# Graph and expert network: the first tile of layer 2 splits its chunks ahead, and layer 1 clamps the rows

## The reference

```
x = x + gnn(layernorm(x));   x = x + ffn(layernorm(x))

gnn(h):  two layers of
    agg[n] = max over the edges (s -> n) of h[s]       # segment_max, 512 wide
    h      = relu(agg @ W_rel.T + b + h @ W_root.T)

ffn(x):  8 experts; each expert takes the 512 nodes with the largest
    softmax(x @ Wr, axis=0), runs gelu(sel @ W1 + b1) @ W2 + b2 (width 256),
    weights the rows and adds them into the output
```

## Time and profile before

| | |
|---|---|
| runs | 989.93, 992.68, 992.88 us; median 992.68 |
| profiled execution | 991.74 us, span of the engines' work 989.9 us |
| busy share of the span | TensorE 70%, VectorE 68%, GpSimd 57%, ScalarE 26% |
| granted TensorE clock, mean | 0.879 of full speed |
| L846, gathers | 372, 393.9 us busy |
| L1165, the sums | 1165 matmuls, 303.3 us busy |
| L899, L910 | 219.2 and 158.1 us busy |
| layer 1, layer 2 (first to last gather) | about 135 to 403 us, 428 to 753 us |

### The profile page before, as it was taken

One profiled execution on the slowest core, in us unless ns is written; L12 is line 12 of the kernel. 1 busy time (PEld: TensorE's weight loads), 2 busy tenths in 40 slices (PEclk: granted clock), 3 DMA queues, 4 the chain that ended last, 5 costly groups with the idle time before them and its releaser, 6 DMA issues.

```text
span 989.9 us, 9615 instructions
## 1 busy us (share of the span) xinstructions
PE 693.8 (70%) x2488; PEld 313.8 (32%) x2523; DVE 674.0 (68%) x1222; ACT 259.1 (26%) x369; POOL 565.9 (57%) x551
## 2 busy tenths in 40 slices
PE   0319286875887888634588858888886414999997
PEld 0215132332333333211143424334433312444442
DVE  3679947888788878635588878888889695231210
ACT  0265151212222221111243314441332100222222
POOL 5655347777777767543156677567667004456533
PEclk9859687997999999785699979998998755999999
DMA  5716537766777766563257777677666604557646
GB/s 139 229 17 211 161 104 207 216 199 186 213 215 205 216 197 201 183 194 113 69 170 214 223 213 239 195 214 238 197 178 178 225 0 111 101 89 116 137 48 80
DMA packets 65780, 164.33 MB, mean 166 GB/s; under 512 B 16592, under 2 KB 20988, under 8 KB 65719
## 3 DMA queue, kind: packets, MB, share of 16 engines
q0 software_dynamic: 41440, 126.86, 47.5%
q1 hardware_dynamic: 17006, 17.17, 6.2%
q10 hardware_dynamic: 7288, 19.76, 6.0%
HBM read 144.44 MB, written 19.18 MB: 165 GB/s over the span
## 4 chain that ended last, share of the span: by engine, by line
PE 39%; DVE 27%; issue 14%; DMA 10%; POOL 4%; ACT 4%; DVEq 2%; POOLq 0%; ACTq 0%; SPq 0%
PE pp L1165 10%; DMA mem<-tab,ic 7%; DVE acc L899 7%; PE pp L1489 6%; PE pp L1476 6%; PE prow L1136 6%; DVE weights L910 6%; PE prow L1103 3%; POOL mem L846 3%; PE prow L1124 2%; DVE mem L1346 2%; PE pp L1487 1%; POOL mem L379 1%; PE prow L520 1%; DVE mem L445 1%
## 5 line engine op out<-in xcount | busy, mean ns | idle before, releaser
L846 POOL DMA_INDIRECT mem<-tab,ic x372 | 393.9, 1059 | 223.0 <-issue 118.1
L1165 PE MATMUL pp<-weights,slots 128*128 128x512 bf16 x1165 | 303.3, 407 | 124.6 <-DVE acc L899 65.6
L899 DVE TENSOR_TENSOR acc<-acc,pp 128x1024 f32<-128x1024 f32 x180 | 219.2, 1218 | 55.0 <-PE pp L1165 48.9
L1165 PEld LDWEIGHTS pp<-weights,slots 128*128 128x128 bf16 x1200 | 117.7, 103 | 313.7 <-issue 114.2
L910 DVE TENSOR_TENSOR weights<-weights,mem 128x1024 f32<-128x1024 f32 x129 | 158.1, 1226 | 18.8 <-DVE weights L910 11.9
L1136 PE MATMUL prow<-weights,aggT 128*128 128x512 f32 x160 | 81.3, 635 | 13.7 <-ACT aggT L1213 13.7
L1528 POOL DMA_INDIRECT out<-mem,node_of x32 | 50.3, 1572 | 69.4 <-ACT mem L1506 67.0
L1457 DVE COPY weights<-prow 128x512 f32<-128x512 f32 x32 | 20.8, 687 | 100.7 <-PE prow L1103 100.7
L1124 PE MATMUL prow<-weights,rootT 128*128 128x512 f32 x160 | 74.0, 605 | 0.0
L1489 PE MATMUL pp<-weights,mem 128*128 128x512 f32 x128 | 63.5, 618 | 0.0
L1476 PE MATMUL pp<-weights 128*128 128x512 f32 x128 | 58.2, 609 | 0.9 <-DVE weights L1457 0.9
(11 more groups left out here) (348 smaller groups left out, 761.2 us busy)
## 6 DMA issues: line engine op xcount, KB each, us to landing
slots<-ttd ACTq DMA_DIRECT2D x20, 640.0 KB, 6.2
mem<-tab,ic POOLq DMA_INDIRECT x372, 3.7
weights<-in_L_ffn_W SPq DMA_DIRECT2D x9, 512.0 KB, 10.7
weights<-in_L_ffn_W ACTq DMA_DIRECT2D x7, 512.0 KB, 4.1
xnd<-xin ACTq DMA_DIRECT2D x10, 256.0 KB, 3.2
mem<-in_x SPq DMA_DIRECT2D x2, 1120.0 KB
tab<-mem SPq DMA_DIRECT2D x1, 2240.0 KB
weights<-in_L_gnn_W_rel SPq DMA_DIRECT2D x2, 1024.0 KB, 12.1
```

The lines of the kernel that those rows point to most:

```text
L846: g.indirect_dma_start(ring[:, h * PAIR + k, :], None, tables[l], bass.IndirectOffsetOnAxis(ic[:, j * PAIR + k:j * PAIR + k + 1], 0))\
L899: v.tensor_tensor(acc[:, :, :], acc[:, :, :], pp[j % 2][:, :, :], ALU.max).then_inc(S["pa"], 1)
L1165: ins = t.matmul(pp[j % 2][:, i, :], sel[u][:, j * KP + i, :], hot[:, j, w, :], start=w == 0, stop=w == 2)
```

## The change

- In layer 2's first tile the loop takes, in round j, what is left of chunk j+3 (`rest`), the third part of chunk j+2 and the maximum of chunk j. Four chunks are begun ahead of it, three of them to the end. The three last gathered pairs are folded after rounds 6, 7 and 8 (before: ahead of maximum 5, ahead of maximum 8, and behind maximum 9).
- The first part is rounded by ScalarE (`high` in `middles`), two chunks ahead of the middle parts.
- The minimum against the largest finite bfloat16 leaves that tile. In layer 1 VectorE does it on the hidden rows (`clamp`), after maximum 2 of the next tile, and writes the clamped rows into `stage`; the tenth clamp stands behind layer 1's last tile. The scatters read `stage` and wait for the clamp (`hc`).
- SP loads the first two blocks of layer 2's index columns ahead of its wait for the scatters.

```diff
@@ SP, per layer
             if l == 0:
                 s.wait_ge(S["xs"], 16 * NQ)
                 after(s, ct, n_wraw)
             else:
+                for b in range(2):
+                    s.wait_ge(s_ic[0][b], (n_pairs_s // LAP) * 16 + 16)
+                    load_indices(0, b)
                 s.wait_ge(S["sc"], 16 * NQ)
...
-            for b in range(2):
-                after(s, ca, n_idx1s[b])
-                if l:
-                    s.wait_ge(s_ic[0][b], (n_pairs_s // LAP) * 16 + 16)
-                load_indices(0, b)
-            after(s, ca, n_idx1)
+            if l == 0:
+                for b in range(2):
+                    after(s, ca, n_idx1s[b])
+                    load_indices(0, b)
+                after(s, ca, n_idx1)
@@ GpSimd, the scatter
-                    g.wait_ge(S["h"], q + 1)
-                    g.indirect_dma_start(tab2, ..., own_row[q], None)\
+                    g.wait_ge(S["hc"], q + 1)
+                    g.indirect_dma_start(tab2, ..., stage[:, q, :], None)\
                         .then_inc(S["sc"], 16)
@@ VectorE
-            def high(c):
-
-                v.wait_ge(s_hx[HGROUP[c]], 32)
-                v.tensor_scalar(hot[0:CN, c, 0, :], stage[0:CN, c, :], TOP, None, ALU.min).then_inc(S["hh"], 1)
+            def clamp(q):
+
+                v.wait_ge(S["h"], q + 1)
+                v.tensor_scalar(stage[:, q, :], own_row[q], TOP, None, ALU.min).then_inc(S["hc"], 1)
+
+            def rest(c):
+
                 v.wait_ge(S["hh"], c + 1)
-                v.scalar_tensor_tensor(stage[0:CN, c, :], stage[0:CN, c, :], TOP, hot[0:CN, c, 0, :], ALU.min, ALU.subtract)\
-                    .then_inc(S["hr"], 1)
+                v.tensor_tensor(stage[0:CN, c, :], stage[0:CN, c, :], hot[0:CN, c, 0, :], ALU.subtract).then_inc(S["hr"], 1)
@@ vec_tile, k == NQ
-                    high(0)
-                    high(1)
+                    rest(0)
+                    rest(1)
                     lowest(0)
-                    high(2)
+                    rest(2)
                     lowest(1)
+                    rest(3)
+                    lowest(2)
                     first_three(k, lo)
-                    pe_pair(k, 1)
-                    for j in range(2, PAIRS):
-                        if j + 1 < NC:
-                            high(j + 1)
-                        lowest(j)
-                        if j == 5:
+                    for j in range(1, PAIRS):
+                        if j + 3 < NC:
+                            rest(j + 3)
+                        if j + 2 < NC:
+                            lowest(j + 2)
+                        pe_pair(k, j)
+                        if j == 6:
                             with v.Fori(3, m) as i:
                                 pool_pair(lo + i)
+                        if j == 7:
+                            pool_pair(lo + m)
                         if j == 8:
-                            pool_pair(lo + m)
-                        pe_pair(k, j)
-                    pool_pair(lo + m + 1)
+                            pool_pair(lo + m + 1)
@@ vec_tile, layer 1, between maximum 2 and maximum 3
+                        if q:
+                            clamp(q - 1)
                         pe_pair(k, 3)
@@ VectorE, behind layer 1's tiles
+            if l == 0:
+                clamp(NQ - 1)
@@ ScalarE
             def middles():
 
-                for c in range(NC):
+                def high(c):
+                    a.wait_ge(s_hx[HGROUP[c]], 32)
+                    a.activation(hot[0:CN, c, 0, :], stage[0:CN, c, :], ACT.Copy).then_inc(S["hh"], 1)
+
+                def middle_part(c):
                     a.wait_ge(S["hr"], c + 1)
                     a.activation(hot[0:CN, c, 1, :], stage[0:CN, c, :], ACT.Copy).then_inc(S["hm"], 1)
+
+                high(0)
+                high(1)
+                for c in range(NC):
+                    middle_part(c)
+                    if c + 2 < NC:
+                        high(c + 2)
```

More of the change, by code:

```diff
@@ L246, in build @@
         names = """x dst small dnx gt gfree gedge gmax edge general w fw fw2 tab src dstf rec recs xs
-            ready done fin rT rTe aT aTe gn h sc xin x2 xn nT nTe lg lge xns bn rc ra fb2 b2 b2l hh hr hm hl nmx exp
+            ready done fin rT rTe aT aTe gn h sc xin x2 xn nT nTe lg lge xns bn rc ra fb2 b2 b2l hc hh hr hm hl nmx exp
             apart_s warm apart_g apart_v out add neg bits bias pairs pa merge mask
@@ L772, in build, with load_indices @@
             features = tables[l][0:N, :].rearrange("n (p j) -> p n j", p=P)
+            def load_indices(i, b):
+                s.dma_start(ic[:, b * SLOTS:(b + 1) * SLOTS], idx1[:, bass.ds((i * 2 + b) * SLOTS, SLOTS)])\
+                    .then_inc(s_ic[l][b], 16)
             if l == 0:
@@ L792, in build @@
                 n_pairs_s = s.value_load(meta1[0:1, NQ:NQ + 1], min_val=NQ * MINP // 2, max_val=NQ * LCAP // 2)
-            def load_indices(i, b):
-                s.dma_start(ic[:, b * SLOTS:(b + 1) * SLOTS], idx1[:, bass.ds((i * 2 + b) * SLOTS, SLOTS)])\
-                    .then_inc(s_ic[l][b], 16)
-            for b in range(2):
-                after(s, ca, n_idx1s[b])
-                if l:
-                    s.wait_ge(s_ic[0][b], (n_pairs_s // LAP) * 16 + 16)
-                load_indices(0, b)
-            after(s, ca, n_idx1)
+            if l == 0:
[3 more added lines that the diff above has]
+                after(s, ca, n_idx1)
             if l:
@@ L860, in build @@
                 for q in range(NQ):
-                    g.wait_ge(S["h"], q + 1)
-                    g.indirect_dma_start(tab2, bass.IndirectOffsetOnAxis(nodeo[:, q:q + 1], 0), own_row[q], None)\
+                    g.wait_ge(S["hc"], q + 1)
+                    g.indirect_dma_start(tab2, bass.IndirectOffsetOnAxis(nodeo[:, q:q + 1], 0), stage[:, q, :], None)\
                         .then_inc(S["sc"], 16)
@@ L1079, in build @@
                 vec_tile(l * NQ + q)
-            if l:
+            if l == 0:
+                clamp(NQ - 1)
+            else:
                 cv.link(v.tensor_scalar(j15[:, :], jji[:, :], J - 1, None, ALU.bitwise_and))
```

## The result

The changed kernel takes 965.21 us (median of four runs, 964.32 to 965.55) where the kernel before takes 992.54 (four runs); the ratio is 0.9729, 95% interval 0.9711 to 0.9747. Predicted were 968.0 and a range of 962.5 to 974. The profiled execution took 965.24 us; its span is 963.4 us, 26.5 us shorter than the span of before.

The account below looks back on a forecast made before the run. The prediction took mutual waits of VectorE and TensorE in layer 2's first tile as the bound. Tile 23.8 plus landing 1.1 minus clamps 0.2 gave 24.7 us, so 992.68 - 24.7 = 968.0, range 962.5 to 974.

Parts of the forecast that it names:

- The ring: Layer 2's first tile: VectorE and TensorE wait for each other in turn, 5.79 us a round, VectorE working 3.0.
- VectorE's chain: Layer 2's first tile, L928 to merge: VectorE's instructions start to start sum to 23.42 us, against the old 47.51.
- the choice between chains: Layer 2's first tile: the longer chain decides, 23.4 or 24.1 us by clock level; 23.7 taken, 23.8 less.
- TensorE's chain at the low clock: Layer 2's first tile: seven chunks at 2.72 us, 24.1 in all; 15 with the fast clock.
- ScalarE's rounding: Layer 2's first tile: first part rounded on ScalarE; left on VectorE, its chain would be 2.8 us longer.
- The landing: Between the layers: the third gathered pair, awaited at L928, lands 1.1 us sooner, bounds 0 and 4.
- The first gather: Start of layer 2: with index columns loaded sooner, gathers can start at about 427.0, 1.5 us sooner.
- The path ahead of L918: Ahead of layer 2's L916 (before): splits ready at 438.7, L916 ends at 439.9, hidden behind the third pair.
- The clamps: Layer 1: nine clamps of 0.42 us ahead of maximum 3, mostly in idle time, cost 0.2 in all, 0 to 10.
- Nothing was given back: After layer 2's first tile: later phases shift whole; rival, a later wait returns the tile's gain, 992.7, chance 0.02.
- the rival that the gathers become the bound: Layer 2: gathers get dearer and bound it; at 1.9 us each, 20 us slower, 1013; chance 0.02.
- The rival with the gathers in full: Layer 2's first tile: L928 starts 4 us sooner and VectorE's chain alone decides, 964.8; chance 0.11.

Follow-up runs that it names:

- the kernel with two rounds first: Changed kernel with rounds 1 and 2 of layer 2's first tile ahead of the wait for the second and third gathered pair: 961.49 us, ratio 0.9696.

## Why the prediction was right

**The ring was what bounded the tile, and the lead opens it.** The prediction took the first tile for a ring in which neither engine is full. The kernel before with the longer lead alone loses 21.96 us of the stretch, and the changed kernel without the lead is back at 46.46. Both sides of the same edit agree.

**VectorE's chain was counted 0.64 us too long, and the choice between chains added 0.28.** Counted were 23.42, taken 23.7, measured 22.78. A gathered pair costs 1.14 until the next start where it stands in this order (459.52 to 460.66), not the 1.25 of the earlier trace rows, three times; the last maximum to the merge 1.36 (465.79 to 467.15), not 1.48; a round 2.34, not 2.36. TensorE's chain at the low clock, 24.1, didn't come about: a chunk took 1.47 us, as in the earlier trace rows, and the granted clock of the stretch is 0.85. Only behind the long wait, after 7.18 us in which TensorE did nothing, did it run low: 0.50 for the 2.72 us from 447.98, chunk 3's sums. Chunks 3 and 4, twelve matmuls, together took 4.34 us, and from 452.65 on the clock is 1.00. The Trainium skill (TensorE: Matmul & The Clock Gate, HAM oscillation) has TensorE stay warm where its work far outlasts its waits, and start cold where a long wait comes again and again. The trace agrees with the direction: 1.47 us of work to waits of 0.72 to 1.40 at clock 1.00, against 2.72 to 3.07 at 0.59 before.

**ScalarE's rounding** was priced at 6 x 0.46 = 2.8 us of VectorE's chain. Taking it back costs 2.76. The Trainium skill's advice to use VectorE for max, min and the like (ScalarE: Activation LUTs, Rules for kernel authors), taken over to this rounding, would have lost that. The advice goes by the time per element, in which the trace agrees (0.42 against 0.63 us); but here VectorE had no room, and ScalarE was busy 10.61 of 22.78 us.

**The landing moved by 1.86 us, where 1.1 was taken.** The term was mis-sized, inside its bounds of 0 and 4. The prediction took 0.6 off the feature rows' start for the last clamp. Its hand-off does cost 0.47, but the last scatter, which reads `stage` and waits for VectorE, takes 3.02 us from its start to its landing, where it took 3.51. This is its line in the chain that ended last:

```profile
423.61 3.02 DMA tab<-weights,nodeo
```

So nothing is left of the delay: the feature rows start 1.39 sooner, not 0.6. The other kernels bear it out. Without clamps the last scatter starts 0.27 or 0.28 us after the hidden rows and lands 3.5 later; with them it starts after 0.73 or 0.74 and lands 3.0 to 3.2 later; with the clamps done twice it starts after 1.19 and lands 2.72 later. The landing comes 3.7 to 3.9 us after the hidden rows each time. What sets it, and so why the clamp in front costs next to nothing, was not tried. The first gather was right: it starts 1.43 sooner, where 1.5 was taken. The path ahead of L918 was shorter than counted, 15.18 us after the last hidden rows, where 16.94 had been counted; L918 waited last for its gathers, 0.48 us, and not for a split. It was hidden behind the third pair, as the prediction had it.

**The clamps** were put at 0.2 us for nine. All nine stand ahead of maximum 3. In seven tiles VectorE still waits 0.24 us for TensorE's sums behind the clamp; in the other two, where it hardly waited before, no idle time is left. One of each:

```profile
193.11 0.43 DVE L935 TENSOR_SCALAR weights<-mem 128x512 f32<-128x512 f32 x1 [1.00 <-ACT mem L1229]
193.78 2.54 DVE L901 TENSOR_TENSOR acc<-acc,pp 128x1024 f32<-128x1024 f32 x2 [0.24 <-PE pp L1176]
...
260.08 0.42 DVE L935 TENSOR_SCALAR weights<-mem 128x512 f32<-128x512 f32 x1
260.42 2.54 DVE L901 TENSOR_TENSOR acc<-acc,pp 128x1024 f32<-128x1024 f32 x2
```

Where the tiles are steady, the clamps cost 0. The sum for layer 1 can't be split finer than about 2 us: kernels that differ in nothing there have 254.78, 256.50 and 256.74. That chance of layer 1 took back 1.1 us of the profiled gain up to the last hidden rows (-0.48 + 2.39 - 0.80).

**Nothing was given back.** The step from merge to next tile is 4.26 us in both, and from there to layer 2's last final maximum the two differ by 0.54 us. GpSimd's 32.0 us of waiting for places in the ring of pairs fell to 4.7, and the rival that the gathers become the bound didn't happen. The rival with the gathers in full, 964.8, is nearer to the measured 965.21 than the forecast is, and half of it is right: VectorE's chain alone decides. Its other half, L928 4 us sooner, isn't; that its number fits is chance.

**The sum.** The stages that the change touches give 24.73 + 1.86 = 26.6 us, against 24.9 predicted before the 0.2 for the clamps. The medians fell by 27.3. The result lies 2.8 us below the forecast. In the spans, the tile gave 0.93 more than forecast and the landing 0.76; layer 1 took back 0.91 (it gave 1.11 away, where 0.2 was forecast), and 1.02 came in the stretches behind, which the change doesn't touch. The last 0.97 is that the forecast put the median 0.94 above the profiled execution, where it came out 0.03 below. So 1.7 of the 2.8 are terms of the change that were mis-sized, and the rest is chance. What isn't settled: by ratios the lead gives 23.6 us, the index columns 3.9, and together 27.5, as much as the whole change, which leaves nothing for ScalarE's 2.76; with intervals of 1.4 to 1.8 us to either side of each, the ratios don't contradict the profile, and don't confirm it. The profile's own sum closes: 21.96 for the lead and 2.76 for the rounding make 24.72 of the tile's 24.73.

## What to carry to other kernels

When two engines are each busy half of a stretch and each waits for the other, count the round in the order of time, and find what the later one does only just ahead of the other's need. Here preparing it two rounds sooner, with buffers already there, was worth the whole difference between the round and VectorE's own work (5.79 to 2.79 us, with the rounding still on VectorE; a lead of one round was not tried). Moving the rounding off VectorE gave 0.45 a round on top of that; with the old lead it shortened a round by as much, but with the folds in their new places the stretch fell only from 47.51 to 46.46. The next step is in the same place: the idle wait for data ahead of the loop, 5.09 us, can hold the first rounds, which don't need that data.

## What the runs showed of the hardware

The kernel before took 992.5 us beside the changed kernel and 992.3 in the second set, but 1063 and 1083 in the first and third, on other chips. In the changed kernel's profiles VectorE's and GpSimd's instructions are as long in the third set as at first (the maximum 1217 ns in both, the gathers 1048 and 1060), TensorE's mean clock is near (0.875 against 0.897), and in the profiles of all sets the part behind the layers is nearly the same (226 to 230 us on the slower chips, 225 to 226 on the others). The difference is in the layers: layer 1 takes 287 to 300 us on the slower chips and 255 to 257 on the others, layer 2's nine later tiles 292 to 309 and 265 to 268. These are the changed kernel's costliest groups in the third set, busy, mean ns of one, idle time and what ended it:

```profile
L848 POOL DMA_INDIRECT mem<-tab,ic x372 | 389.7, 1048 | 289.9 <-issue 140.5 <-DVE weights L912 97.8 <-SPq L815 27.1
...
L901 DVE TENSOR_TENSOR acc<-acc,pp 128x1024 f32<-128x1024 f32 x180 | 219.1, 1217 | 89.4 <-PE pp L1176 38.8 <-remote 35.5 <-issue 9.1
```

The idle time ahead of L901 is 89.4 us, of which 35.5 is put down to no instruction that the profile holds ("remote"); in the profile after it is 24.9 in all. What causes it was not tried.

On ScalarE two passes start 0.52 to 0.54 us apart (431.14 and 431.68) though each lasts 0.61 to 0.63, so two of them in a row cost less than their durations. On VectorE it is the same: 0.60 us from start to start for a duration of 0.68, and 1.13 to 1.14 for 1.21.

TensorE's granted clock also fell in a gap much shorter than the 7.18 us ahead of chunk 3. In the kernel with two rounds first, the chunks at 441.69 and 444.03 ran at clock 1.00 (441.69 to 445.50), and the chunk at 447.87, after 2.37 us of idleness, at 0.50 (447.87 to 450.59).
